# One product instead of four for the gates of the delta rule, in a kernel whose order of work is written out and redrawn

## The reference, cut to what matters

```
beta = jax.nn.sigmoid(x @ Wb)
g = x @ Wg + bg
hg = x @ Wh + bh
w = jax.nn.softmax(jnp.stack([g, hg, jnp.zeros_like(g)], -1), -1)
w_l, w_g, w_r = (w[..., 0], w[..., 1], w[..., 2])
```

## Time and profile before

| | |
|---|---|
| time, median of 3 runs | 1239.53 us (1236.46 to 1243.86) |
| time of the profiled execution | 1239.64 us, of which the span is 1238.2 us |
| PE busy | 1161.1 us, 94% of the span |
| PEld busy | 922.5 us, 75% |
| DVE busy | 913.7 us, 74% |
| POOL busy | 840.4 us, 68% |
| ACT busy | 707.2 us, 57% |
| HBM traffic | 228.9 MB, read and written |
| chain that ended last | 57% PE, 22% DVE, 10% ACT, 4% issue, 3% DMA, 2% POOL |

### The profile page before, as it was taken

How to read it: one execution, slowest core, us unless ns; L and a number is a source line. 1 busy time by engine, 2 the same in 40 slices (tenths; PEclk the granted TensorE clock), 3 DMA queues, 4 the chain that set the end, 5 groups by cost and what they waited for, 6 DMA issues and landing times.

```text
span 1238.2 us, 31062 instructions
## 1 busy us (share of the span) xinstructions
PE 1161.1 (94%) x11890; PEld 922.5 (75%) x11890; DVE 913.7 (74%) x1902; ACT 707.2 (57%) x2020; POOL 840.4 (68%) x1156
## 2 busy tenths in 40 slices
PE   5887789999999999999999999999999999899998
PEld 3454458877778788787887877987788877788786
DVE  4958786986888978885687787986677766784534
ACT  5787877656756564467645665457775533332322
POOL 3745467687688845799488726798669736873871
PEclk9889989999999999999999999999999999999999
DMA  7101165654366665773477556685257666777763
GB/s 267 35 23 52 33 225 183 211 193 157 117 192 206 208 198 172 250 253 115 168 234 242 180 165 197 230 280 165 94 161 228 227 205 242 237 249 250 262 225 125
DMA packets 91186, 230.87 MB, mean 186 GB/s; under 512 B 9888, under 2 KB 16160, under 8 KB 90912
## 3 DMA queue, kind: packets, MB, share of 16 engines
q1 hardware_dynamic: 90896, 228.30, 56.3%
q10 hardware_dynamic: 144, 0.59, 0.1%
HBM read 225.71 MB, written 3.15 MB: 185 GB/s over the span
## 4 chain that ended last, share of the span: by engine, by line
PE 57%; DVE 22%; ACT 10%; issue 4%; DMA 3%; POOL 2%; DVEq 0%; SPq 0%; ACTq 0%; POOLq 0%
PE bank L948 13%; PE bank L901 12%; PE bank L612 5%; PE bank L829 4%; DVE ogate L1358 4%; PE bank L938 3%; PE bank L919 3%; DVE dy L1211 2%; PE bank L647 2%; PE bank L929 2%; DMA kv<-values 2%; DVE kv L1125 2%; PE bank L671 2%; ACT prob L1469 2%; PE bank L657 1%
## 5 line engine op out<-in xcount | busy, mean ns | idle before, releaser
L1744 POOL TENSOR_TENSOR vgate<-vgate,xT 128x512 f32<-128x512 f32 x256 | 325.7, 1298 | 72.0 <-DMA vgate<-gates 67.3
L901 PE MATMUL bank<-wv,vgate 128*128 128x128 f32 x2048 | 252.6, 277 | 1.6 <-POOL vgate L1744 1.0
L901 PEld LDWEIGHTS bank<-wv,vgate 128*128 128x128 f32 x2048 | 242.4, 192 | 13.4 <-issue 7.8
L948 PE MATMUL bank<-ogate,wo 128*128 128x256 f32 x1024 | 242.7, 383 | 2.1 <-DVE ogate L1358 1.7
L948 PEld LDWEIGHTS bank<-ogate,wo 128*128 128x128 f32 x1024 | 188.5, 190 | 33.0 <-issue 8.9
L1358 DVE TENSOR_TENSOR ogate<-ogate,bank 128x1024 f32<-128x1024 f32 x128 | 153.4, 1212 | 34.6 <-PE bank L938 28.3
L1469 ACT ACTIVATE prob<-prob,mx 128x128 f32<-128x128 f32 (+1 forms) x256 | 96.0, 377 | 47.6 <-DVE mx L1061 47.2
L1628 ACT ACTIVATE mprob<-bank,mmin 128x256 f32<-128x256 f32 x128 | 59.4, 469 | 107.5 <-DVE mmin L1347 106.9
L1676 POOL TENSOR_TENSOR rot<-rot 128x512 f32<-128x512 f32 x64 | 82.0, 1281 | 55.2 <-DVE rot L1037 54.9
L612 PE MATMUL bank<-wqkv,hT 128*128 128x512 f32 x192 | 107.0, 661 | 2.9 <-ACT hT L1405 1.9
L1721 POOL TENSOR_TENSOR dlt<-dlt,step 128x126 f32<-128x126 f32 (+22 forms) x248 | 93.3, 376 | 19.4
(11 more groups left out here) (224 smaller groups left out, 2385.5 us busy)
## 6 DMA issues: line engine op xcount, KB each, us to landing
ogate<-gates SPq DMA_DIRECT2D x128, 512.0 KB, 4.2
vgate<-gates SPq DMA_DIRECT2D x128, 512.0 KB, 4.0
wo<-in_wo_moe SPq DMA_DIRECT2D x128, 256.0 KB, 4.6
wv<-in_wv_moe SPq DMA_DIRECT2D x128, 256.0 KB, 4.5
kv<-values SPq DMA_DIRECT2D x64, 256.0 KB, 4.7
local<-in_local SPq DMA_DIRECT2D x1, 1715.0 KB, 9.4
wqkv<-in_wqkv SPq DMA_DIRECT2D x2, 768.0 KB, 6.4
x<-in_x SPq DMA_DIRECT2D x8, 128.0 KB, 5.3
```

What stands on the lines that cost most here:

```text
L901: i = nc.tensor.matmul(out[:, n * D:(n + 1) * D], xg[:, e, n * P:(n + 1) * P], m.wv[slot][:, e, :], start=(q, n, e) == (0, 0, 0), stop=(q, ...
L948: i = nc.tensor.matmul(out[:, 0:T], m.wo[slot][:, e, :], cg[:, e, :], start=(h, q, e) == (0, 0, 0), stop=(h, q, e) == (MH - 1, 1, EQ - 1))
L1744: i = tt(gate[:, e:e + half, :], gate[:, e:e + half, :], spread(m.xT[b % 2][:, :], 1, half), ALU.mult)
```

## The change

The 16 gate columns are laid out anew: for each head 32 columns, of which the first four are the head's four gates and 28 are zero. One product of 128 rows and 256 columns then makes all gates of all heads, and one transposition of 32x32 blocks puts a head's four gates side by side on each token's partition. `de` gets a tile of its own, so `dgT` is only the gates' and DVE's `dgate` no longer waits for the front. The tile `dg` has two parts instead of four. All six strings of the order are drawn anew.

```diff
-    "layer1": {"w_delta": (P, 3, D), "conv": (P, 3, CONV), "w_gate": (P, 4, P), "gate_b": (P, 2), "dnorm": (P, CH), "wo_delta": (P, D),
+    "layer1": {"w_delta": (P, 3, D), "conv": (P, 3, CONV), "w_gate": (P, P), "gate_b": (P, 2), "dnorm": (P, CH), "wo_delta": (P, D),
...
-    return ticks + [[("dgate", b, 0)], [("dgate", b, 1)], [("dgates", b)]]
+    return ticks + [[("dgate", b)], [("dgates", b)]]
...
-        sb("dgT", 4, NC_, CH), sb("dg", 4, NC_), sb("dm", NC_)
-        self.de = self.dgT[:, :, :, :].rearrange("p a c t -> p a (c t)")[:, 0:3, :]
+        sb("de", 3, T), sb("dgT", NC_, CH), sb("dg", 2, NC_), sb("dm", NC_)
...
-    def dgate(b, k):
-        bank = banks.of("dgate", b, k)
+    def dgate(b):
+        bank = banks.of("dgate", b)
         out = take(bank)
         x_ready(b)
-        for i in range(2):
-            last = nc.tensor.matmul(out[:, i * T:(i + 1) * T], m.w_gate[:, 2 * k + i, :], m.xT[b % 2][:, :],
-                                    start=True, stop=True)
-        last.then_inc(bank.filled, 1)
+        nc.tensor.matmul(out[:, 0:T], m.w_gate[:, :], m.xT[b % 2][:, :], start=True, stop=True).then_inc(bank.filled, 1)
...
-    def dgate(b, k):
-        bank = banks.of("dgate", b, k)
-        out = filled(bank)
-        v.wait_ge(s.yn, nth("l2", b))
-        nc.vector.transpose(m.dgT[:, 2 * k:2 * k + 2, :, :].rearrange("p a b c -> p (a b c)"), out).then_inc(bank.emptied, 1)
+    def dgate(b):
+        bank = banks.of("dgate", b)
+        nc.vector.transpose(flat(m.dgT), filled(bank)[:, 0:T]).then_inc(bank.emptied, 1)
...
-        v.chain(tt(dg[:, 2:4, :], m.dgT[:, 2:4, :, 0], spread(m.gate_b[:, :], 2, NC_), ALU.add))
+        v.chain(tt(dg[:, :, :], m.dgT[:, :, 2:4].rearrange("p c g -> p g c"), spread(m.gate_b[:, :], 2, NC_), ALU.add))
...
-        act(m.gates[b % 2][:, 0:2, :], m.dgT[:, 0:2, :, 0], ACT.Exp, scale=-1.0).then_inc(s.dbeta_raw, 1)
+        act(m.gates[b % 2][:, 0:2, :], m.dgT[:, :, 0:2].rearrange("p c g -> p g c"), ACT.Exp, scale=-1.0).then_inc(s.dbeta_raw, 1)
...
-    a["w_gate"] = np.repeat(w_gate, CH, 1).reshape(D, 4, DH * CH)
+    w_gate = w_gate.reshape(D, 4, DH).transpose(0, 2, 1)
+    a["w_gate"] = np.pad(w_gate, ((0, 0), (0, 0), (0, CH - 4))).reshape(D, DH * CH)
```

Of the tables a line shows the kind of difference:

```diff
 TENSOR_TURNS = (
-    "GaaaaGGGaaaaaXabbabbaGbbbaababGbbabacaaacbGbGGaccabGcbbaaabbGbGbGaabGbaaabbbcabacbbbcbcbbGcbbaGbacacGaaaacacbG"
+    "GaaaaGGGaaaaaXabbabbaGbbbabaabGbbabacaaacbGbGGaccabGcbbaaabbGbGbGaabGbaababbcabacbbbcbcbbGGcbbabaaccGaaaaacbbc"
```

More of the change, by code:

```diff
@@ L88 @@
[L88 to L92, removed]
@@ L120 @@
     "AEAAAAAAAAAAAAAAAAAAAAAAAAAAAAADDE")
 GPSIMD_TURNS = (
[L123 to L126, removed]
@@ L137 @@
+    "oovoovvoovvoovvoooooE")
 BANK_TURNS = (
[L138 to L141, removed]
@@ L151 @@
+    "23074107251340251034250345203472354203574207652073562073506750362753065276052376052036570236236352362705627065"
+    "06753673563567367516735163156156371501627041623416203650234610532615024351042361425641254615423145231054613705"
+    "26417506427106524107562471056741650461750641507")
 PACKS = {
@@ L1237, in dgates @@
         v.chain(nc.vector.reciprocal(beta, beta))
-        bank = banks.of("dgate", b, 1)
+        bank = banks.of("dgate", b)
         v.wait_ge(bank.emptied, bank.use)
-        v.chain(tt(dg[:, 2:4, :], m.dgT[:, 2:4, :, 0], spread(m.gate_b[:, :], 2, NC_), ALU.add))
+        v.chain(tt(dg[:, :, :], m.dgT[:, :, 2:4].rearrange("p c g -> p g c"), spread(m.gate_b[:, :], 2, NC_), ALU.add))
         v.settle()
-        v.chain(tt(dm, dg[:, 2, :], dg[:, 3, :], ALU.max))
+        v.chain(tt(dm, dg[:, 0, :], dg[:, 1, :], ALU.max))
         v.settle()
@@ L1245, in dgates @@
         v.settle()
-        v.chain(tt(w3[:, 0:2, :], dg[:, 2:4, :], spread(dm, 1, 2), ALU.subtract))
+        v.chain(tt(w3[:, 0:2, :], dg[:, :, :], spread(dm, 1, 2), ALU.subtract))
         ts(w3[:, 2, :], dm, -1.0, None, ALU.mult).then_inc(s.dw_raw, 1)
@@ L1566, in fT @@
         if b >= 2:
-            for read in (banks.of("dgate", b - 2, 1), banks.kept("scores", b - 2, MH - 1)):
+            for read in (banks.of("dgate", b - 2), banks.kept("scores", b - 2, MH - 1)):
                 a.wait_ge(read.filled, read.fill)
@@ L1594, in dgates @@
     def dgates(b):
-        bank = banks.of("dgate", b, 0)
+        bank = banks.of("dgate", b)
         a.wait_ge(bank.emptied, bank.use)
-        act(m.gates[b % 2][:, 0:2, :], m.dgT[:, 0:2, :, 0], ACT.Exp, scale=-1.0).then_inc(s.dbeta_raw, 1)
+        act(m.gates[b % 2][:, 0:2, :], m.dgT[:, :, 0:2].rearrange("p c g -> p g c"), ACT.Exp, scale=-1.0).then_inc(s.dbeta_raw, 1)
         w3 = m.gates[b % 2][:, 2:5, :]
```

88 lines of the change are left out of this document (48 added, 40 removed).

## The result

The changed kernel takes 1232.34 us, the median of 15 runs (1224.83 to 1240.52); the kernel before takes 1241.8 us beside it (15 runs, 1236.46 to 1251.91). The ratio is 0.9928, with a 95% interval of 0.9906 to 0.995, so 8.9 us or 0.72% less. The profiled execution of the changed kernel took 1234.39 us, with a span of 1233.1 us.

What follows compares the result with a forecast made beforehand. PE was taken as the bound, though not everywhere (94% busy, 57% of the chain). Products -7.7 to -10.4, DVE 0 to -0.7 and order 0, from 1239.64 us, gave 1228.5 to 1231.9, taken as 1230; range 1220 to 1241 us.

Steps and rivals of the forecast that it cites:

- The products that go: On PE, 24 of 32 gate products go, at 0.4325 us each: -7.7 to -10.4 us.
- three quarters of 10.2 us: Lower end for the products: ten chain pieces of gate products sum to 10.2 us, three quarters of them 7.7 us.
- The order: All six strings redrawn: priced at 0, bounds -4 to +3 us at the first sample and 9 us either way later.
- Rival C: Freed 10 us turn into waits for other engines: 4.5 us lost, 1234 up to 1243 us, typical 1237; chance 0.27.
- The transpositions: DVE does 8 of 128x256 instead of 16 of 128x512: 7.8 us less on DVE, 0 to -0.7 us in the chain.
- What is free: Smaller pack of weights, a bank taken once per sample, DVE's wait for the front's end gone: priced at 0.
- The first sample: Choice of experts in one piece, 8.7 us on DVE; gates sent before 158 us, first `hv` between 170 and 178 us.
- The wait of 2.8 us: PE was to wait about 2.8 us at the first sample's transposition of the choice's result.
- Idle time as the judge of A, B and C: PE's idle time in the profile after: near 77 us for A, 5 or more below for B, 83 and above for C.
- A: The forecast itself: products' time comes back, order as good as before, 1230 us within 1226 to 1234; chance 0.50.
- B: Order also gives back two first-sample waits (3.7 us) and a clock fall (2.6 us): 1224, down to 1218 us; chance 0.15.
- rival D: Slower by the clock: PE's wait at the first sample leaves work behind it at 1.2 GHz, 1246 to 1250 us; chance 0.08.

Runs made afterwards that it cites:

- four_products: Changed kernel in its new order, each sample's gate product issued four times into the same place, against the kernel before: 1239.39 us, ratio 0.9995.
- three_turns: Changed kernel with DVE's transposition of the gates issued three times for each sample: 1236.03 us, ratio to before 0.9957, 3.6 us above the changed kernel.
- cut_old_order: The changed kernel's code in the order of before, with only the second gate stage and its bank dropped: 1240.71 us, ratio to before 0.9996.
- warm4: Changed kernel with four useless identity products ahead of PE's wait in each of 32 stages of samples 0 and 1: 1238.5 us, ratio to before 0.997.
- warm2: Changed kernel with two useless identity products ahead of PE's wait in each of 32 stages of samples 0 and 1: 1234.19 us, ratio to before 0.994.

## Why the prediction came out, point by point

The time was forecast as 1230 us and measured as 1232.34, or 0.9928 against a forecast of 0.9922. The number came out; two of the steps beneath it hold only together, which the prediction didn't see, and that is in part luck.

- **The products that go**, -7.7 to -10.4 us. In the new order right: 24 products are worth 8.3 us there, and 72 more cost 35 us. As it was put, though, as a property of the kernel before ("three quarters of 10.2 us"), it is wrong: in the order of before the runs give 0.5 to 2.0 us, none of it told from nothing. The chain of before did pass through ten gate pieces, but what a chain shows is where the end came from in that execution. With a piece shorter, another wait can take its place, as at 769 us and at the last `lp`. The price of one product, 0.4325 us, stands: in the profiles, PE of `four_products` is busy for 1164.1 us, 10.5 more than the 1153.6 of the changed kernel.
- **The order**, 0. With PE's work held as before it is worth 2.1 us at the medians (1.0012 to 0.9995), which the intervals don't tell from nothing. With the work cut it is worth 8.4 us (the intervals leave 4 to 13), since it is what lets the cut through. The step that does not hold is adding the two as if each had a price of its own. It came out because the sum was taken along the one path on which both figures hold: first the order at full work, 0, then the cut in the new order, -8.3. Along the other path, first the cut and then the order, the same steps would read -0.5 and -8.4. Nothing in the prediction chose the path for this reason: with another redrawn order the same sum would have stood there.
- **Rival C**, the freed time turns into waits, was given 0.27 and 4.5 us of loss. Its mechanism is there, and stronger than it was put: in the old order it eats nearly all or all. The change escapes it by its redrawn strings. The prediction took this rival's size from the shares of the chain (43% of 10.4 us), and the runs in the old order show that it can't be read there.
- **The transpositions.** Their cost on DVE, 0.44 us, was right to 10 ns on the mean. That they are worth next to nothing in the end was neither shown nor refuted by `three_turns`.
- **What is free**, 0. The freed bank, the tile of its own and the smaller pack of weights are all in `cut_old_order`, which shows no gain; in the new order they were not tried by themselves.
- **The first sample.** The gates left before 158 us and the first `hv` came within 170 to 178 us, as said; the choice's chain was under 10 us. The wait of 2.8 us did not come, since PE's work ahead of it was costed at the full clock in a stretch where the mean was 0.70.
- **Idle time as the judge of A, B and C.** It was to be near 77 us for A, and is 79.5; PE's busy time near 1151, and is 1153.6. The extra 2.6 us of busy time go with a lower clock late in the program, of which the text said that no wait brought it down from 300 us on (rival D's last sentence). That was true of the kernel before and is not of this one.

## What the runs showed that I had not expected

In the kernel before, no slice of 3 us behind 300 us has a granted clock under 0.99. The changed kernel falls to 1.2 GHz four times there. Three of the four come behind its three longest waits of PE in that part:

```profile
499.09 0.70 PE L876 MATMUL bank<-dsq,layer 128*128 128x256 f32 x2 [2.77 <-DVE dsq L1322]
...
1017.86 0.33 PE L824 MATMUL bank<-state,winvT 32*32 32x32 f32 x16 [2.14 <-DVE state L1304]
...
1078.62 0.66 PE L924 MATMUL bank<-small,mprob 128*128 128x128 f32 x4 [2.08 <-ACT mprob L1628]
```

```profile
357.00:360.00 3.00, 3.00 (x12) 2.55 (x11) 2.79 (x9) 1.34 (x8) 2.50 (x3) 0.54 0.02 5
...
501.00:504.00 3.00, 3.00 (x8) 2.37 (x9) 2.86 (x8) 0.63 (x1) 0.00 (x0) 0.50 0.03 5
...
1020.00:1023.00 3.00, 3.00 (x13) 2.69 (x12) 2.73 (x5) 0.00 (x0) 3.00 (x3) 0.53 0.19 62
1080.00:1083.00 3.00, 2.88 (x11) 2.57 (x12) 2.89 (x6) 1.37 (x2) 2.53 (x7) 0.64 0.31 115
```

The first, at 357 us, follows on two waits close together (1.17 us at 354.99 and 0.68 at 356.70). In each such slice PE is busy almost throughout, and the DMA share is down, to 0.02 and 0.03 in two of them; I take it, without having tried it, that loads wait there for buffers that a slow PE has yet to free. The kernel before has the same wait for `dsq`, but of 1.91 us, and keeps its clock. Here it is 0.9 us longer, and half of some 3 us is lost behind it as well. The length of one wait doesn't decide it, though. `four_products` fell to a granted clock of 0.51 from 1023 us on, behind a wait of 1.85 us at 1021.98, and `warm4` kept 1.00 from 1020 to 1032 us with this one in it:

```profile
1024.55 0.33 PE L830 MATMUL bank<-state,winvT 32*32 32x32 f32 x16 [2.12 <-DVE state L1310]
```

The Trainium skill (TensorE: Matmul & The Clock Gate, the section HAM oscillation) says that waits between bursts of products put the clock back. In the kernel before, whose longest wait from 300 us on is 1.91 us, nothing of that shows; the three falls of the changed kernel agree with it, and the row of `warm4` is one such wait that did not.

Among the 15 runs of the changed kernel the time goes with the mean granted clock: the six fastest (1224.83 to 1229.68 us) have 0.982 or 0.983, and the five slowest (1236.41 to 1240.52 us) 0.974 to 0.978; the four between do not keep to it (1232.34 us has 0.976, 1233.74 has 0.982). That the falls cause the spread of 16 us was not tried: the runs with added products raised the clock in the first 155 us and left falls from 300 us on (`warm2` still has three), and their mean clock (0.984 in `warm2` against 0.980) brought no time. So a higher mean clock is not by itself less time. Removing the three waits behind 300 us is the version that I would try next, and it hasn't been run.

## What to carry to other kernels

Where the order of each engine's work is fixed, a cut of the busiest engine's work may have no price of its own: in this kernel the same 24 products were worth 8.3 us in one order and 0.5 to 2.0 us in the other, while the order was worth little without the cut. So before a cut that gives nothing is dropped, try it with a redrawn order (here one was tried; that any redrawing would do is not shown). And to see where it went, don't compare busy and idle time in stretches of one length, but the start of the same product in both traces: here, in the old order, some 3 us were won up to 750 us and lost again by 877, at waits for engines that hadn't become faster. And cost work in a stretch at the clock that the stretch shows, not at the full one.
